# Order of the work rewoven, one more turn on TensorE, bf16 parts made by GpSimd, in an attention and FFN kernel

## The chip, the cores and the metric

One core of a Trainium2 chip. The metric is the device time of one execution in microseconds, the median over runs of the same program.

## The reference

`x` is 2 x 1024 tokens of 128 channels. All is float32.

```python
xn = layernorm(x)                                   # no gain, no bias, eps 1e-5
# attention, 8 heads; queries and keys have 3 channels a head, values 16
q3, k3 = (xn @ Wq.T), (xn @ Wk.T)                   # (b, t, h, 3)
v = xn @ Wv.T                                       # (b, t, h, 16)
scores = q3 . k3 * scale + (q3 . dirs) (k3 . dirs)  # dirs: a fixed unit vector a head
scores = where(causal, scores, -inf)
attn = softmax(scores) @ v;  attn_out = attn @ Wo.T
# FFN, 128 -> 512 -> 128, with ternary weights and a low-rank term
h = xn @ (ternary(w_fc) * s_fc).T + gate * (xn @ v_.T @ fast_b.T @ u.T)
out = x + attn_out + (relu(h) ** 2) @ (ternary(w_proj) * s_pj).T
```

## The kernel before

The 2048 tokens are four **quarters** of 512 (quarter q, half of a batch). The attention runs in eight **chunks** c: one batch, one group of four heads, one block of 512 queries (`CHUNKS`). In the order of `CHUNKS`, chunks 0, 1, 6 and 7 have queries in the first half of their batch (four key tiles, all on the diagonal), chunks 2 to 5 in the second half (eight key tiles, the last four on the diagonal). Quarters 0 and 1 are closed by chunks 1 and 3, quarter 3 by chunk 5 and quarter 2 by chunk 7.

For queries and keys, f32 values are split into three bf16 parts (high, middle, low), which are spread with repeats into rows of the SBUF tile `X` (18 copies of 288 elements in all by GpSimd, line L426); `X` is turned into `QK`, in which the rows of a head lie along the partitions, and one bf16 matmul of 32 rows gives scores of nearly f32 exactness. For quarter 0 TensorE and ScalarE turn it (items `rows`), for quarters 1 to 3 a DMA transpose on SyncE's queue (L355). The split of a later quarter before the change: ScalarE casts PSUM to the high part (L695), VectorE subtracts that from PSUM into an f32 rest in SBUF (L544), GpSimd casts the rest to the middle part (L415) and subtracts for the low one (L416).

For each chunk, TensorE makes the scores a first time with queries along the partitions (`max`, L922) and VectorE takes the row minima of the negated scores (L588 whole, L591 with the causal mask); GpSimd splits these maxima into three bf16 parts and writes them into X beside the queries (`prep`, L464 to L467). X of the chunk's queries is then turned once more (`maxT`): for chunks in `TURNED` by four matmuls with the identity into a PSUM bank (L933) and a ScalarE copy (L726), for the others by a DMA transpose on SyncE (L364). After it TensorE makes the scores with keys along the partitions (`st`, L950), which have the maximum subtracted already; ScalarE applies relu on the diagonal block (`late`, L743) and exp (L757), GpSimd cuts the diagonal block (`causal`, L454), and TensorE multiplies with V (`pv`, L973) into one bank. VectorE and GpSimd then normalise (`oT` L615, `norm` L444), VectorE turns (`oB` L627), and TensorE adds the attention's projection (L993, `y`) to the FFN's (`hid`, L791) in the same bank; VectorE adds x (L634) and SyncE sends the result (out_y, L372). FFN: `ffn`/`ffn2` (L897, L902), relu on ScalarE (L737), `square` on GpSimd (L434). `ternary` (L407 to L410) makes ternary weights on GpSimd, item 0 for w_fc and item 1 for w_proj.

**The order** of all this is one list, `ORDER`. It is written out by hand in the string `WEAVE`: each letter stands for the next item of the stream with that letter in `streams()` (M maxima, A `st`, O `late`, G exp, D `causal`, P `pv`, B `hid`, Y outputs, R `prep`, T `maxT`, I `split`, L `spread`, J ternary 1, S square, n `norm`, E rows, K an idle matmul on zeros). Every engine and SyncE walk through the list and issue, in order, what is theirs; semaphores hold an item until its inputs are there. PSUM has three banks of ring `v` (maxima, weights, turns, FFN output) and two double banks of ring `a` (`st`, `qkv`, `ffn`, xT); units take the banks of their ring in the order of the list.

SyncE's part of the list, before the change, is: rows 1, maxT 1, rows 2, maxT 2, rows 3, maxT 3, maxT 4, y of quarter 0 (first half), maxT 5, y of quarter 0 (second half), maxT 6, y of quarter 1 twice, maxT 7, y of quarter 3 twice, y of quarter 2 twice.

## Time and profile before

| | |
|---|---|
| time, median of 3 runs | 167.89 us (167.42 to 167.95) |
| the profiled execution | 167.61 us, span 165.8 us |
| mean granted TensorE clock | 0.986 |
| TensorE busy | 150.2 us (91%) |
| VectorE busy | 127.1 us (77%) |
| ScalarE busy | 124.1 us (75%) |
| GpSimd busy | 70.7 us (43%) |
| chain that ended last | TensorE 50%, ScalarE 25%, VectorE 7%, issue 7%, DMA 4%, SyncE 3% |

The profile is of one execution. Times are us from the start of the span unless marked ns. A row of an order of time gives start, duration, engine, line, operation, output<-input, form, count, and in brackets how long the engine had been idle before it and what released it. PE is TensorE, PEld its weight loads, DVE VectorE, ACT ScalarE, POOL GpSimd, SPq SyncE's queue. PEclk is the granted clock, 1.00 for 2.4 GHz and 0.50 for 1.2 GHz.

### The profile page before, as it was taken

To read this page: it belongs to the slowest core of one execution; us is meant where nothing else is said; L and a number is where in the kernel's file an instruction comes from. 1 tells how busy PE (TensorE), PEld (TensorE's weight loads), DVE (VectorE), ACT (ScalarE), POOL (GpSimd) and SP (SyncE) were. 2 spreads that over 40 slices of the span, in tenths; PEclk is the share of its full clock that TensorE was granted. 3 is DMA by queue.
4 is the path that set the end of the run, shared out by engine and by line. 5 is a ranking of instruction groups with operands and counts; after the bars stand their busy time and mean duration, and the time that the engine had idled before them with its cause. 6 is when DMAs were issued, how large, how long until landed. Compare 5 with 4: busy or idle time off the path is not lost.

```text
span 165.8 us, 3297 instructions
## 1 busy us (share of the span) xinstructions
PE 150.2 (91%) x1105; PEld 64.2 (39%) x1109; DVE 127.1 (77%) x423; ACT 124.1 (75%) x222; POOL 70.7 (43%) x126
## 2 busy tenths in 40 slices
PE   6999899999999998999899989998499999869992
PEld 2464543523232423213132122234163255655682
DVE  5887899899999999999999979995386873111152
ACT  0888793589789879887899897887399989656700
POOL 4064029649777996157003830045016333411420
PEclk9999999999999999999999999999999999987998
DMA  3850000601042101501000100000202000210022
GB/s 94 202 177 0 6 2 2 124 0 32 4 86 44 32 0 30 101 0 31 4 0 0 34 4 2 0 4 0 63 0 54 14 0 0 62 37 2 0 67 65
DMA packets 16621, 5.71 MB, mean 34 GB/s; under 512 B 11292, under 2 KB 16476, under 8 KB 16604
## 3 DMA queue, kind: packets, MB, share of 16 engines
q1 hardware_dynamic: 16208, 5.34, 14.0%
q8 instruction: 9, 0.15, 0.4%
q10 hardware_dynamic: 396, 0.16, 0.4%
q14 instruction: 8, 0.07, 0.1%
HBM read 1.96 MB, written 1.05 MB: 18 GB/s over the span
## 4 chain that ended last, share of the span: by engine, by line
PE 50%; ACT 25%; DVE 7%; issue 7%; DMA 4%; SPq 3%; ACTq 1%; POOLq 0%; POOL 0%; DVEq 0%
ACT Pr L757 18%; PE obank L973 8%; PE vbank L791 8%; PE vbank L922 7%; PE abank L950 6%; PE abank L897 5%; PE abank L902 5%; DVE vbank L591 5%; ACT abank L743 4%; PE obank L798 3%; DMA QK<-X 3%; PE abank L878 3%; ACT r L737 2%; PE vbank L993 2%; DMA v_sb<-in_L_ffn_v 1%
## 5 line engine op out<-in xcount | busy, mean ns | idle before, releaser
L757 ACT ACTIVATE Pr<-abank 128x1024 f32<-128x1024 f32 (+3 forms) x96 | 74.8, 815 | 13.1 <-PE abank L950 7.1
L591 DVE CUSTOM_DVE_ANT_0 vbank<-vbank,mask_row 128x128 f32<-128x128 f32 (+3 forms) x128 | 59.0, 523 | 10.0 <-PE vbank L922 8.3
L922 PE MATMUL vbank<-QK 32*128 32x512 bf16 (+2 forms) x192 | 40.1, 328 | 1.0 <-DVE pm L591 0.7
L588 DVE TENSOR_REDUCE pm<-vbank 128x1 f32<-128x512 f32 x64 | 39.7, 682 | 1.5 <-PE vbank L922 0.9
L973 PE MATMUL obank<-Pr,V 128*32 128x512 f32 (+3 forms) x384 | 39.7, 498 | 0.1
L454 POOL TENSOR_SCALAR_AFFINE_SELECT Pr<-Pr 128x512 f32<-128x512 f32 x32 | 20.3, 638 | 40.4 <-ACT Pr L757 40.2
L950 PE MATMUL abank<-QK 32*128 32x512 bf16 (+3 forms) x192 | 30.1, 333 | 8.0 <-DMA QK<-X 5.1
L743 ACT ACTIVATE abank<-abank 128x256 f32<-128x256 f32 x64 | 23.7, 376 | 7.8 <-PE abank L950 7.4
L922 PEld LDWEIGHTS vbank<-QK 32*128 32x128 bf16 x192 | 11.7, 91 | 35.7 <-issue 16.6
L950 PEld LDWEIGHTS abank<-QK 32*128 32x128 bf16 x192 | 8.4, 91 | 31.1 <-ACT Pr L757 18.2
L791 PE MATMUL vbank<-w2T,r 128*128 128x128 f32 x128 | 18.6, 298 | 0.2 <-DVE pm L591 0.2
L591 DVE DVE_READ_ACCUMULATOR2_ANT pm<- 128x1 f32 x128 | 18.1, 142 | 0.0
L791 PEld LDWEIGHTS vbank<-w2T,r 128*128 128x128 f32 x128 | 16.3, 203 | 2.2 <-issue 0.9
L434 POOL TENSOR_TENSOR r<-r 128x1024 f32<-128x1024 f32 x8 | 15.1, 1895 | 0.2
L798 PE MATMUL obank<-mask_row 128*128 128x512 bf16 x43 | 13.8, 422 | 1.5 <-POOL mask_row L386 1.3
L444 POOL TENSOR_TENSOR on<-oT,inv 128x256 f32<-128x256 f32 x8 | 5.0, 622 | 21.3 <-DVE inv L618 21.3
L615 DVE STREAM_TRANSPOSE oT<-obank 128x512 f32<-128x512 f32 x8 | 5.7, 713 | 8.9 <-PE obank L973 8.9
L973 PEld LDWEIGHTS obank<-Pr,V 128*32 128x32 f32 x384 | 8.3, 109 | 10.7 <-issue 8.5
L737 ACT ACTIVATE r<-abank 128x1024 f32<-128x1024 f32 x8 | 8.2, 1024 | 4.2 <-PE abank L902 4.2
L897 PE MATMUL abank<-xnT,w1T 128*128 128x512 f32 x16 | 8.9, 638 | 0.4 <-ACT Pr L757 0.2
L634 DVE TENSOR_TENSOR xn<-vbank,x_sb 128x256 f32<-128x256 f32 x8 | 3.3, 415 | 7.4 <-PE vbank L993 7.4
L902 PE MATMUL abank<-xnT,w1T 128*128 128x512 f32 x16 | 9.0, 645 | 0.0
(111 smaller groups left out, 125.4 us busy)
## 6 DMA issues: line engine op xcount, KB each, us to landing
x_sb<-in_L_attn_x SPq DMA_DIRECT2D x4, 256.0 KB, 3.5
out_y<-xn SPq DMA_DIRECT2D x8, 128.0 KB, 1.9
wfc_sb<-in_L_ffn_w_fc SPq DMA_DIRECT2D x1, 256.0 KB, 3.6
wpj_sb<-in_L_ffn_w_proj SPq DMA_DIRECT2D x1, 256.0 KB, 2.8
QK<-X SPq DMA_TRANSPOSE x10, 2.4
k_sb<-in_consts SPq DMA_DIRECT2D x1, 64.0 KB, 2.8
Wv_sb<-in_L_attn_Wv ACTq DMA_DIRECT2D x1, 64.0 KB, 3.4
Wo_sb<-in_L_attn_Wo ACTq DMA_DIRECT2D x1, 64.0 KB, 3.8
```

What stands on the lines that cost most here:

```text
L454: nc.gpsimd.affine_select(diagonal, diagonal, [[0, HG], [1, P]], ALU.is_ge, 0.0, base=0, channel_multiplier=-1).then_inc(causal_done, 1)
L588: last = nc.vector.tensor_reduce(out=least, in_=s_n, op=ALU.min, axis=AX.X)
L591: last = nc.vector.tensor_tensor_reduce(out=s_n, in0=s_n, in1=mask_row[:, CH - keys:CH], scale=1.0, scalar=3.0e38, op0=ALU.add, op1=ALU.mi ...
L743: nc.scalar.activation(scores, scores, ACT.Relu).then_inc(bounded, 1)
L757: nc.scalar.activation(Pr[:, n % PSLOTS, 2 * pair:2 * pair + 2, 0:cols], src[:, :, 0:cols], ACT.Exp, scale=-1.0).then_inc(free(unit), 1)
L791: nc.tensor.matmul(o[:, at:at + P], r2[:, j, t:t + P], w2T[:, j, :], start=j == 0 and at == 0, stop=False)
L798: nc.tensor.matmul(obank[:, :], zeros[:, 0:P], zeros, start=True, stop=True)
L897: nc.tensor.matmul(o[:, 0, :], w1T[:, j * P:(j + 1) * P], xnT[:, q * CH:(q + 1) * CH], start=True, stop=True)
L902: nc.tensor.matmul(bank(unit)[:, 1, :], w1T[:, j * P:(j + 1) * P], xnT[:, q * CH:(q + 1) * CH], start=True, stop=True).then_inc(full(unit), 1)
L922: last = nc.tensor.matmul(o[:, at:at + keys], QK[r, quarter(b, chunk), 0, g, q0:q0 + P], QK[r, quarter(b, half), 1, g, 0:keys], start=True ...
L950: last = nc.tensor.matmul(o[:, n, 0:cols], QK[r, quarter(b, j // TPC), 1, g, k0:k0 + P], QK[r, quarter(b, chunk), 0, g, first:CH], start=T ...
L973: last = nc.tensor.matmul(obank[32 * h:32 * h + 32, first:CH], V[:, b * TPB + j, HG * g + h, :], Pr[:, n % PSLOTS, h, 0:cols], start=step ...
```

## The change

- `TURNED` gains chunk 7: its maxima are turned by four matmuls and a ScalarE copy, no DMA.
- For quarters 1 to 3 ScalarE copies queries and keys from PSUM to the f32 rest in SBUF; GpSimd casts it to the high part and subtracts (two instructions more a quarter, in its chain), and then goes on as before. VectorE's subtraction goes, and V's copy by ScalarE (L708) has no wait for it.
- `WEAVE` is another order of the same 653 items. SyncE's part becomes: rows 1, maxT 1, maxT 2, rows 2, rows 3, maxT 3, maxT 4, maxT 5, y of quarter 0 (first half), y of quarter 0 (second half), maxT 6, y of quarter 1 twice, y of quarter 3 twice, y of quarter 2 twice.
- TensorE from chunk 5's last maxima matmul to its first scores, before: st, pv 4.3, st, two max, hid, two st, hid, two max, st, y, st, pv 4.4 (4.3 and 4.4: steps 3 and 4 of chunk 4). After: st, pv 4.3, st, two max, st, hid, st, hid, st, one max, st, y, one max.
- TensorE from chunk 6's first scores to chunk 7's: before, the other seven st, hid of quarter 1 three times, pv 5.6 and 5.7, y, pv 6.0, y, one hid of quarter 3. After: two max, hid of quarter 1 (all four now), st, pv 5.6, 5.7, st, hid, st, hid, st, y, maxT 7, hid, two st, hid 3, y, st. Chunk 7's last maxima are the two max.
- GpSimd, before, from chunk 1's prep: squares 1 and 2, causal 0.0, square 3, causal 0.1, spread 2, further causal items, square 4, prep 2, ternary 1, three causal, split 3, spread 3, norm 0. After: split 2 ahead of prep 1; from it square 0, ternary 1, spread 2, causal 0.0 and 0.1, square 1, causal 0.2, prep 2, four causal items, square 2, split 3, causal 1.3, norm 0, spread 3, square 3. The last square, ahead of causal 5.0 before, comes between causal 6.0 and 6.1.
- Idle matmuls: 47 before and after; ahead of the first chunk's maxima 27 before and 23 after, ahead of chunk 2's 32 and 28, ahead of quarter 3's xT 33 and 39.

```diff
--- before.py
+++ after.py
@@ -100,7 +100,7 @@
 
 
 
-TURNED = (0,)
+TURNED = (0, 7)
 
 
 def own(c):
@@ -163,12 +163,12 @@
 
 
 WEAVE = """
-KKKKKKKKNKKWKKNCNNWKKXWFUQKNKKKIKKLNUKEVKFKKKNCKKMNMNEKKMMNUMMXKJKMMNMQHNMMVIMHMMXMMLHMMRHEMMQTVMMHMMHSAMOIKMG
-MMHRMMHMAMMSKSOGXMMKKAMOGMHMMAOGMHMMKMAAMDKOKGMMOAOKKSDMGKMAKTGAMOGMLDKMKMAOKGOGDAMMKSKAMODGMMOPMEAMGAOMPGMORJ
-DMAGAOOPGTPGDPMMAQMAMVPDMIMAMAMPLAMMJMAMMAPMAEnMPAMMHPnOMGAMOGHMMMPMAAMOMGOPAGMOMPGMAORDMMAOGPMGMAOSHDMGTAMDHM
-MMAADMMPAMMAMPAMMAMPPAPMMMAOPGAMOMMGAOPMnGDMAPOMGMRAOPDGAMOMMGAOSPGADMMOGTADMAPMAMPAMMAMPHPMMMAHPMMAAMPMAMMMOA
-GMPMOMAGPMAMMDOBGAOGYnRAOBOMGMGAOYGTAODPGAAMMDMPPDAMPMPMnABAMABAMYMAPAROMSMGAPMMAPOGMOMGDAOPMGDAOMPGAOTMMGMAPD
-OAGBOGMAOAYBOBMGGADPPDPROAGYAOGPABOGOAYDTGOAGOGBAOADOBGGBAOPDAPnPGAOGDOYDPBGAPPAOnGDOABYOGGYPDPBPnYBBYY
+NKKKKKNKWKCKKKKKNWKKNXWUFQNILKUKKVKEKKNNKEKKCNMMFNUKJMMHMNHMXMKMMQMMMHNMVMHMXKMMMQMMNVIHMLEMRITHMMKAMKMOHRMGMM
+KHMMSAKKMOKMJKMAMGAKMLOGKKMMODAKGMOHGMAOMMDHGMSMKTMKXMMAKOKGAMKDAMKOMMGOAMKKGAMKMKMOMGAOMRGOPDGMAMOAMPGDOMGMTA
+APODPMMODSGGAQPMVMMIAPAMAMPMMDAPAMPnMEAMMPHAMMHMPMAAMOMLOMSPGGMADEAMOMMnGOPGAMMSOMAPOGMMGMAROHMGMAOHMTDGMJMAAM
+DMPMAMMDAPMAMMAPPAPMMnMAPAMAMMPMOMOGAMGPMOAGOARDMOMGGPAMMOMADPGAMOTGOGMADAMMPMDAMAMPPAMMMAMHAPMHMMPAMAMMPMAMMO
+PGOMGAOMGPADMMABOYGAROGBAOMGDOAOTDYGGMAAMMPMAMDPMAMPPAMnMSAMBAMRMPABAOYAGPnAOMMMGPTSOAMPMGMOAYPMMGOADGAOOGDGPP
+DAAMMOMBOGAGDOPPGRAOBABGDOAYGOGTBSAAOBPYODGGAOADOPGPnGAABODOGBAGPOGPAYOPBDGYAOAYBGnDOAPPDPOGGDPPnBBYBYY
 """
 
 
@@ -411,7 +411,9 @@
                 elif item[0] == "split" and item[1]:
                     q = item[1]
 
-                    pool.wait_ge(res_ready, q + 1)
+                    pool.wait_ge(hi_ready, q + 1)
+                    link(nc.gpsimd.tensor_copy(bf16_part(q, 0), rest(q)))
+                    link(nc.gpsimd.tensor_tensor(rest(q), rest(q), bf16_part(q, 0), ALU.subtract))
                     link(nc.gpsimd.tensor_copy(bf16_part(q, 1), rest(q)))
                     nc.gpsimd.tensor_tensor(bf16_part(q, 2), rest(q), bf16_part(q, 1),
                                             ALU.subtract).then_inc(lo_ready, 1)
@@ -535,14 +537,11 @@
                                                 ALU.subtract, ALU.mult).then_inc(xn_ready, 1)
                 elif item == ("weights", "wqk"):
                     nc.vector.tensor_copy(wall[:, C:VQK], filled(item)[:, 0:2 * NQ]).then_inc(free(item), 1)
-                elif kind == "qkv":
-                    q = item[1]
-                    src = qkv_view(item)[:, :, C:VQK].rearrange("p t (s c) -> p t s c", s=2 * G) if q else qk_rest()
-
-                    dve.wait_ge(hi_ready, q + 1)
-
-                    nc.vector.tensor_tensor(rest(q) if q else src, src, bf16_part(q, 0),
-                                            ALU.subtract).then_inc(res_ready, 1)
+                elif item == ("qkv", 0):
+                    dve.wait_ge(hi_ready, 1)
+
+
+                    nc.vector.tensor_tensor(qk_rest(), qk_rest(), bf16_part(0, 0), ALU.subtract).then_inc(res_ready, 1)
                 elif item == ("split", 0):
                     dve.wait_ge(mid_ready, 1)
                     nc.vector.tensor_tensor(bf16_part(0, 2), qk_rest(), bf16_part(0, 1),
@@ -692,7 +691,9 @@
                     else:
                         filled(item)
                         src = qkv_view(item)[:, :, C:VQK].rearrange("p t (s c) -> p t s c", s=2 * G)
-                    nc.scalar.copy(bf16_part(q, 0), src).then_inc(hi_ready, 1)
+
+
+                    nc.scalar.copy(rest(q) if q else bf16_part(q, 0), src).then_inc(hi_ready, 1)
                 elif kind == "v":
                     q = item[1]
                     unit = ("qkv", q)
@@ -703,7 +704,6 @@
                         act.wait_ge(ones_ready, 2)
                         src = filled(unit)[:, 0, :].rearrange("p (n h d) -> p n h d", n=TPC, d=HD)
                     else:
-                        act.wait_ge(res_ready, q + 1)
                         src = qkv_view(unit)[:, :, 0:C].rearrange("p n (h d) -> p n h d", d=HD)
                     nc.scalar.copy(V[:, q * TPC:(q + 1) * TPC, :, 0:HD], src).then_inc(free(unit), 1)
                 elif item == ("split", 0):
```

## Rows read from the trace of the kernel before

**Rows 1.** Busy time by stage: window; length, busy us (x instructions); PEclk, DMA share, GB/s.

```profile
core 0: us, PE busy (x) PEld busy (x) DVE busy (x) ACT busy (x) POOL busy (x), PEclk, DMA share, GB/s
...
35.00:50.00 15.00, 14.61 (x73) 4.54 (x72) 14.86 (x42) 13.04 (x22) 12.68 (x18) 1.00 0.19 38
50.00:65.00 15.00, 13.92 (x122) 5.09 (x122) 14.72 (x39) 13.10 (x23) 13.38 (x22) 1.00 0.09 18
...
118.20:134.10 15.90, 15.63 (x147) 5.87 (x147) 12.65 (x49) 14.32 (x21) 4.84 (x9) 1.00 0.07 18
134.10:144.40 10.30, 10.30 (x91) 7.14 (x89) 3.59 (x10) 9.00 (x20) 4.13 (x10) 1.00 0.04 13
```

**Rows 2.** Order of time, around the first wait of TensorE for a turn.

```profile
111.80 0.27 POOL L467 TENSOR_TENSOR X<-nres,X 128x16 bf16<-128x16 f32 x1
...
114.06 0.23 PE L950 MATMUL abank<-QK 32*128 32x128 bf16 x2
...
114.22 1.06 PE L973 MATMUL obank<-Pr,V 128*32 128x512 f32 x8
...
115.19 0.40 SPq L372 DMA_DIRECT2D out_y<-xn  x1
...
115.64 1.21 SPq L364 DMA_TRANSPOSE QK<-X  x1
...
118.21 0.40 PE L950 MATMUL abank<-QK 32*128 32x512 bf16 x4 [2.93 <-DMA QK<-X]
```

**Rows 3.** Order of time around the second wait, and the clock (window of TensorE alone).

```profile
135.85 2.05 PE L791 MATMUL vbank<-w2T,r 128*128 128x128 f32 x16
...
139.87 0.28 POOL L467 TENSOR_TENSOR X<-nres,X 128x16 bf16<-128x16 f32 x1
...
144.09 1.20 SPq L364 DMA_TRANSPOSE QK<-X  x1
...
146.64 0.40 PE L950 MATMUL abank<-QK 32*128 32x512 bf16 x4 [2.21 <-DMA QK<-X]
...
146.97 3.23 PE L791 MATMUL vbank<-w2T,r 128*128 128x128 f32 x16
...
148.00:149.00 1.00, 1.00 (x7) 0.50 0.00 0
```

**Rows 4.** Order of time, the turn of chunk 0 by TensorE and ScalarE.

```profile
30.41 0.39 PE L933 MATMUL vbank<-k_sb,X 128*128 128x128 bf16 x4
...
30.84 0.59 ACT L726 CAST QK<-vbank 128x512 bf16<-128x512 f32 x1
```

**Rows 5.** Order of time of ScalarE: start and end of chunk 6, last exp of chunk 7.

```profile
135.70 0.65 ACT L743 ACTIVATE abank<-abank 128x256 f32<-128x256 f32 x2 [0.22 <-PE abank L950]
...
143.87 0.38 ACT L757 ACTIVATE Pr<-abank 128x256 f32<-128x256 f32 x1
...
156.57 0.67 ACT L757 ACTIVATE Pr<-abank 128x256 f32<-128x256 f32 x2
```

**Rows 6.** By source line: duration ns min/median/max, first and last start us.

```profile
L544 DVE TENSOR_TENSOR r<-abank,r x3: 354/357/358, 23.2 to 58.9; 128x192 f32<-128x192 f32 x3
...
L415 POOL CAST r<-r x3: 344/344/345, 23.7 to 60.6; 128x192 bf16<-128x192 f32 x3
...
L416 POOL TENSOR_TENSOR r<-r x3: 563/564/566, 24.1 to 61.1; 128x192 bf16<-128x192 f32 x3
...
L426 POOL COPY X<-r x18: 433/566/622, 24.8 to 63.9; 128x288 bf16<-128x288 bf16 x18
```

**Rows 7.** Order of time of GpSimd, and what waits for it.

```profile
36.39 3.75 POOL L434 TENSOR_TENSOR r<-r 128x1024 f32<-128x1024 f32 x2
...
51.86 1.06 PE L973 MATMUL obank<-Pr,V 128*32 128x512 f32 x8
...
53.83 1.27 POOL L407 TENSOR_TENSOR on<-on 128x512 f32<-128x512 f32 x1
...
61.77 2.77 POOL L426 COPY X<-r 128x288 bf16<-128x288 bf16 x6
...
72.02 8.44 DVE L588 TENSOR_REDUCE pm<-vbank 128x1 f32<-128x512 f32 x13
```

## The prediction

> **What bounds the kernel now.** I read the stage table first. From 35 to 65 us three engines are nearly full together: between 35 and 50 us TensorE is busy 14.61 of 15.00 us and VectorE 14.86, between 50 and 65 us VectorE 14.72 and GpSimd 13.38 [rows 1]. VectorE makes the row maxima there, and goes on with them to 110 us. After 118 us VectorE thins out (12.65 of 15.90, then far less), and TensorE carries the time: 15.63 of 15.90 us and 10.30 of 10.30 us [rows 1]. In such a stretch a wait of TensorE goes straight to the end.
>
> Then I looked for those waits, by the chain of waits and the order of time. There are two long ones, both for a DMA that turns an X tile into QK.
>
> The first: GpSimd ends the maxima of chunk 5 at 111.80 + 0.27 = 112.07 us, but SyncE issues their turn only at 115.64 us, because out_y of quarter 0, first half, stands ahead of it in SyncE's order, waits for VectorE, and is issued at 115.19 us. TensorE has its next scores only at 118.21 us, after 2.93 us of wait [rows 2]. From issue to scores are 118.21 - 115.64 = 2.57 us.
>
> The second: chunk 7's maxima are ready at 139.87 + 0.28 = 140.15 us; SyncE issues their turn at 144.09 us, behind an out_y, and TensorE goes on at 146.64 us, after 2.21 us [rows 3]. This wait has a second price. In 148 to 149 us the granted clock is 0.50, the lower of the two levels (1.2 of 2.4 GHz), and the sixteen FFN matmuls (L791) in it take 3.23 us where sixteen took 2.05 us at full clock [rows 3]: 1.18 us more. TensorE was full up to 144.4 us and stood still for 2.2 us before the fall. After the first, longer wait that doubling isn't seen: the stage from 118.20 to 134.10 us has clock 1.00 [rows 1]. So I count the clock once.
>
> **The change part by part.**
>
> *Turn of chunk 5 ahead of out_y on SyncE.* The turn can be issued at 112.07 us and serve at 112.07 + 2.57 = 114.64 us. What is late next is TensorE's own order. Before, chunk 4's last scores run at 114.06 us and a PV step from 114.22 to 115.28 us stands before chunk 5's first scores [rows 2]. In the new order that PV step stands behind them, so TensorE is ready at about 114.2 us, and 114.64 - 114.2 = 0.4 us of wait is left. The wait of 2.93 us shrinks to that: -2.5 us (bounds -2.0, if GpSimd or the order before it is later, and -2.9). The out_y transfer, now second, has 50 us to land; nobody waits for it.
>
> *Turn of chunk 7 by TensorE.* One DMA goes, and four matmuls and one ScalarE copy come in. The same turn for chunk 0 is in the trace: four matmuls in 0.39 us and a copy of 0.59 us [rows 4]. Nobody waits for SyncE any more. The maxima are ready 2.5 us or so after their last matmul; in the new order chunk 6's scores, four FFN matmul groups and y come between, and between the turn and its first reader there are two more FFN groups (about 1.1 us each), y and three score pairs, some 3.8 us of TensorE work, against 0.59 us of copy plus at most two queued ScalarE instructions. The wait goes: -2.2 us. The clock's price goes with it: -1.2 us (bounds -0.5, if some fall comes elsewhere, and -1.7, 3.5 us at half rate). The four matmuls lie on the bound engine: +0.4 us (up to +1.0 if the copy counts as well).
>
> Of a TensorE transpose of 128x128 bf16, the Trainium skill ("TensorE: Matmul & The Clock Gate", Part 4: PE-mode transpose) says some 275 ns inside a kernel. Four would be 1.1 us by that, and the time 0.7 us later, 162.9 us; the row has them overlapped in 0.39 us, and this kernel's are plain matmuls with the identity, so the row is taken.
>
> *Is ScalarE the next bound?* Chunk 6's relu and exp run without a gap from 135.70 to 144.25 us, 8.55 us [rows 5]. Chunk 5 took from its first scores at 118.21 us to 135.70 us, 17.5 us [rows 2, 5]. From first scores at about 114.7 us ScalarE needs 17.5 + 8.55 + 0.59 + 8.55 = 35.2 us and ends at 149.9 us, 7.3 us before its present end of 156.57 + 0.67 = 157.24 us [rows 5]. TensorE's gains so far are 2.5 + 2.2 + 1.2 - 0.4 = 5.5 us. ScalarE could follow with 1.8 us to spare; TensorE stays the bound, closely.
>
> *Later parts of queries and keys by GpSimd.* VectorE loses three subtractions of 356 ns, 1.07 us, all inside the stretch in which it is full. The one of quarter 3 (after 50 us) counts whole; the two before 35 us, where I have no row that tells VectorE's bound from TensorE's, half: -0.7 us (bounds 0 and -1.1) [rows 1, 6]. ScalarE's copy now writes f32 instead of bf16, which I cost at nothing, and the PSUM bank comes free without a wait for VectorE. GpSimd gets, three times, the cast (344 ns, as its own cast L415) and a subtraction with an f32 result. The nearest row is L416, 564 ns with a bf16 result; from the squares, 3.75 us for two of 1024 elements, 192 elements would be 0.35 us [rows 6, 7]. I take 0.5 us, so 0.9 us for each quarter with the chain of semaphores. Behind it on GpSimd stand the spread (L426), the causal masks and the maxima of the next chunk; who waits are SyncE's turn of the quarter and the PV steps. Quarter 3's spread ends at 61.77 + 2.77 = 64.5 us, and chunk 4's first maxima, which need its turn, come at 72.02 us [rows 7]. That leaves 7.5 us for a transfer of which a smaller one took 2.57 us to its reader, so 0.9 us is hidden there. Cover gone, it would cost at most its own 0.9 us a quarter.
>
> The projection's ternary work (four instructions in a chain, the first 1.27 us, 5.1 us if all are as long [rows 7]) moves from behind chunk 2's maxima to before quarter 2's spread. With one square less in that part, GpSimd has in 35 to 65 us 26.1 + 1.8 - 1.9 = 26.0 of 30 us [rows 1, 6, 7]. From 36.39 us there stand a square (1.9), the ternary work (5.1) and a spread (2.8) before the first mask (0.6): it is there at about 46.8 us, and the first PV step comes at 51.86 us [rows 7]. No cost; one is a rival below.
>
> A rule of the skill speaks against this part: GpSimd shares its SBUF interfaces with VectorE and contends with VectorE instructions of two SBUF inputs or in a two-port mode ("GPSIMD Engine Reference", Key points). L416 took 563 to 566 ns all three times, but the spread's copies 433 to 622 ns [rows 6], so the trace leaves room for it; its result is the slower rival.
>
> *The rest of the order.* As many fillers as before, fewer of them ahead of the first maxima and more in chunk 2's. The start is bound by the same chain to the first maxima, so 0 us, bounds -1.0 and +1.5, since every join of three full engines is new. For joins in the tail that don't fit as well as they did in 118 to 144 us, I add +0.5 us (0 to 2), by the 0.39 and 1.08 us that TensorE lost in 35 to 50 and 50 to 65 us [rows 1].
>
> **The sum.** -2.5 - 2.2 - 1.2 + 0.4 - 0.7 + 0.5 = -5.7 us. The span 165.8 becomes 160.1 us. The profiled run took 167.61 us, 1.8 us more than its span, and lay 0.28 us under the median of 167.89: 160.1 + 1.8 + 0.3 = 162.2 us.
>
> **Rivals.**
>
> 1. The middle gives part back: joins at their upper bounds (+2 us over the 0 and 0.5 that I took). For it speaks that three engines are full from 35 to 110 us; against, that VectorE has less to do. 164.2 us.
>
> 2. The turn by TensorE comes late: its copy stands in ScalarE's full queue, or GpSimd is late with the maxima, TensorE waits as before and the clock falls again. Then 2.2 + 1.2 us are not won: 165.6 us. Against it stand 3.8 us of work between turn and reader.
>
> 3. The middle wins too: VectorE's full 1.1 us and 1.0 us from the leaner start, no loss at joins: 162.2 - 0.4 - 1.0 - 0.5 = 160.3 us; with the clock's bound of -1.7 it is 159.8 us.
>
> 4. Slower: GpSimd becomes the bound of 35 to 65 us, by contention. If its instructions stretch by the ratio of the spread's copies, 622 / 433 = 1.44, its 26.0 us become 37.4 us in a stretch of 30, and all behind its masks moves by 7.4 us: 162.2 + 7.4 = 169.6 us. It decides from a stretch of 30 / 26.0 = 1.15, and makes the kernel slower than before from (30 + 5.7) / 26.0 = 1.37. The equal durations of L416 speak against it.
>
> 5. The change doesn't do what it says: SyncE's queue still blocks. In the new order chunk 5's turn stands ahead of the first out_y, chunk 6's behind out_y of quarter 0 but 30 steps ahead of its reader; that leaves it next to nothing. About 167.5 us.
>
> **How the numbers follow.** Forecast (160.7 to 163.5 us): 0.66. Rival 1 (up to 165.0): 0.14. Rival 2: 0.05. Rival 3: 0.09. Rival 4: 0.03. Rival 5 and no change: 0.03. The range 159.8 to 164.8 us takes in the forecast, nearly all of rival 1 and two thirds of rival 3, about 0.85. A difference of 0.3% is about what a measurement of this kernel can tell from none. Faster: 0.66 + 0.14 + 0.05 + 0.09 = 0.94; same 0.03; slower 0.03.
>
> **What would show it.** First wait: chunk 5's scores at most 0.5 us after the PE work before them, no SP line between 112 and its turn. Second: no wait for a DMA after 130 us, four matmuls at L933 a second time, clock 1.00 in every slice up to the last. VectorE: one subtraction at the old L544 instead of four, and chunk 5's last maxima some 0.7 us earlier than 110.4 us. GpSimd: six new instructions of 0.35 to 0.6 us, and no PV step waiting for a mask before 65 us. Wrong would be: a new wait of TensorE of over 1 us anywhere, GpSimd durations above those of before, a clock of 0.50 in another place, or a last maximum of chunk 5 later than 111 us.

## The result, and the profile after

The changed kernel takes 159.69 us (median of 4 runs, 159.43 to 160.19); the kernel before, on the same chip, 167.92 us (167.42 to 169.38). The ratio is 0.95, 95% interval 0.9435 to 0.9565. Here and below a median is over all executions, while a ratio leaves out those over 1.5% above the fastest of their kernel, which count as a slower state. The forecast was 162.2 us with a range from 159.8: the direction was right, and the time fell 0.1 us below the range. The profiled execution took 159.43 us with a span of 157.7 us, where the sum had 160.1 us. So 8.1 us of span went, and the sum had 5.7.

The first lines of the page of after, TensorE's clock in 40 slices (9 stands for 0.9 or more), and the only line that the view of TensorE's waits has after 100 us (line waited for: us in total, times, longest):

```profile
span 157.7 us, 3312 instructions
...
PE 148.4 (94%) x1113; PEld 63.7 (40%) x1113; DVE 126.9 (80%) x420; ACT 124.1 (79%) x223; POOL 73.0 (46%) x132
...
PEclk9999999999999999999999999999999999999999
...
PE abank L950 <- ACT Pr L757: 0.9, 3, 0.5
```

TensorE's busy time fell by 1.8 us (from 150.2) and its idle time from 15.6 to 9.3 us. No wait for a DMA is left after 100 us, and the granted clock is 1.00 in every stage of the table below. In the kernel before, the same view had 5.1 us for the DMA of QK, in two waits [rows 2, 3].

Order of time of after, at the places of [rows 2] and [rows 3] (start, duration, engine, line):

```profile
110.50 0.27 POOL L469 TENSOR_TENSOR X<-nres,X 128x16 bf16<-128x16 f32 x1
...
110.79 1.68 SPq L364 DMA_TRANSPOSE QK<-X  x1
...
114.09 0.67 PE L950 MATMUL abank<-QK 32*128 32x512 bf16 x4
...
114.46 9.30 SPq L372 DMA_DIRECT2D out_y<-xn  x2
...
136.52 0.39 PE L933 MATMUL vbank<-k_sb,X 128*128 128x128 bf16 x4
...
137.31 0.58 ACT L726 CAST QK<-vbank 128x512 bf16<-128x512 f32 x1
...
139.53 0.45 PE L950 MATMUL abank<-QK 32*128 32x128 bf16 x4
```

The turn of chunk 5 is issued 0.02 us after its maxima are whole, and its scores follow other work with nothing in brackets, which is to say without a wait. Chunk 7's turn is four matmuls and a copy that ends at 137.89 us, 1.6 us before the scores that first read it.

To see where the time went, I cut both spans at the same events: the last maxima of chunk 0 and of chunk 5, the first scores of chunks 5 and 7, the end of the last PV step. Before, from chunk 4's last maxima on (columns as in [rows 1]):

```profile
90.50:110.56 20.06, 18.65 (x155) 4.51 (x153) 18.42 (x51) 17.33 (x28) 6.39 (x11) 1.00 0.04 8
110.56:118.21 7.65, 4.72 (x40) 2.97 (x41) 3.73 (x19) 4.16 (x11) 3.10 (x8) 1.00 0.15 36
118.21:146.64 28.43, 25.96 (x236) 13.03 (x237) 16.95 (x59) 23.32 (x40) 10.17 (x19) 1.00 0.10 24
146.64:158.76 12.12, 12.12 (x113) 7.87 (x113) 1.82 (x4) 7.76 (x16) 3.13 (x5) 0.86 0.01 2
```

After:

```profile
90.67:109.26 18.59, 17.33 (x149) 4.48 (x145) 18.30 (x52) 16.50 (x26) 4.01 (x9) 1.00 0.05 9
109.26:114.09 4.83, 4.14 (x38) 2.96 (x34) 2.95 (x15) 4.44 (x11) 2.46 (x7) 1.00 0.16 31
114.09:139.53 25.44, 25.22 (x240) 13.06 (x238) 16.94 (x62) 23.23 (x40) 13.29 (x21) 1.00 0.08 22
139.53:151.04 11.51, 11.51 (x124) 7.22 (x123) 2.96 (x6) 8.38 (x19) 4.84 (x8) 1.00 0.12 35
```

| stage | before, us | after, us | difference |
|---|---|---|---|
| start to chunk 0's maxima | 25.93 | 26.03 | +0.10 |
| to chunk 4's maxima | 64.57 | 64.64 | +0.07 |
| to chunk 5's maxima | 20.06 | 18.59 | -1.47 |
| to chunk 5's scores | 7.65 | 4.83 | -2.82 |
| to chunk 7's scores | 28.43 | 25.44 | -2.99 |
| to the last PV step's end | 12.12 | 11.51 | -0.61 |
| to the end | 7.04 | 6.66 | -0.38 |
| span | 165.8 | 157.7 | -8.1 |

Two things stand out. The stretch of 64.6 us in which VectorE lost two of its three subtractions (the first, at 23.2 us [rows 6], lies ahead of chunk 0's maxima) is as long as before. And chunk 5's maxima, of which the prediction said nothing apart from VectorE's 0.7 us, came 1.5 us sooner after chunk 4's, while chunk 4's came 0.5 us later after chunk 3's (19.07 against 18.58 us).

### The profile page after: what moved, and what is told of

The parts are those of the page before. It is cut to its first block, busy times and chain, and to the rows that moved or that the text cites. A ratio compares the mean times of both kernels' runs of the same rounds, so it can differ in the third digit from the quotient of the medians.

```text
span 157.7 us, 3312 instructions
## 1 busy us (share of the span) xinstructions
PE 148.4 (94%) x1113; PEld 63.7 (40%) x1113; DVE 126.9 (80%) x420; ACT 124.1 (79%) x223; POOL 73.0 (46%) x132
## 4 chain that ended last, share of the span: by engine, by line
PE 56%; ACT 24%; DVE 12%; issue 6%; ACTq 0%; POOL 0%; DVEq 0%; POOLq 0%
ACT Pr L757 19%; PE vbank L922 8%; PE vbank L791 8%; PE obank L973 8%; PE obank L798 8%; DVE pm L587 6%; PE abank L897 5%; PE abank L902 5%; ACT abank L743 5%; PE abank L950 4%; DVE vbank L590 4%; PE vbank L993 2%; PE abank L878 2%; PE abank L849 2%; PE vbank L829 1%
## 5 line engine op out<-in xcount | busy, mean ns | idle before, releaser
L590 DVE CUSTOM_DVE_ANT_0 vbank<-vbank,mask_row 128x128 f32<-128x128 f32 (+3 forms) x128 | 58.9, 524 | 6.7 <-PE vbank L922 6.5
L922 PE MATMUL vbank<-QK 32*128 32x512 bf16 (+3 forms) x192 | 40.8, 329 | 2.2 <-DVE pm L590 0.9
L587 DVE TENSOR_REDUCE pm<-vbank 128x1 f32<-128x512 f32 x64 | 39.4, 682 | 0.6 <-PE vbank L922 0.5
L973 PE MATMUL obank<-Pr,V 128*32 128x512 f32 (+3 forms) x384 | 38.6, 495 | 0.2 <-issue 0.2
L950 PE MATMUL abank<-QK 32*128 32x512 bf16 (+3 forms) x192 | 30.6, 331 | 2.0 <-ACT Pr L757 1.6
L590 DVE DVE_READ_ACCUMULATOR2_ANT pm<- 128x1 f32 x128 | 18.3, 143 | 0.0
L798 PE MATMUL obank<-mask_row 128*128 128x512 bf16 x47 | 16.4, 430 | 1.3 <-POOL mask_row L386 1.3
L791 PE MATMUL vbank<-w2T,r 128*128 128x128 f32 x128 | 17.6, 284 | 0.0
L950 PEld LDWEIGHTS abank<-QK 32*128 32x128 bf16 x192 | 8.6, 91 | 21.3 <-ACT Pr L757 15.6
L791 PEld LDWEIGHTS vbank<-w2T,r 128*128 128x128 f32 x128 | 15.3, 191 | 1.9 <-issue 1.2
```

The lines of the kernel that those rows point to most:

```text
L587: last = nc.vector.tensor_reduce(out=least, in_=s_n, op=ALU.min, axis=AX.X)
L590: last = nc.vector.tensor_tensor_reduce(out=s_n, in0=s_n, in1=mask_row[:, CH - keys:CH], scale=1.0, scalar=3.0e38, op0=ALU.add, op1=ALU.mi ...
L791: nc.tensor.matmul(o[:, at:at + P], r2[:, j, t:t + P], w2T[:, j, :], start=j == 0 and at == 0, stop=False)
L798: nc.tensor.matmul(obank[:, :], zeros[:, 0:P], zeros, start=True, stop=True)
L922: last = nc.tensor.matmul(o[:, at:at + keys], QK[r, quarter(b, chunk), 0, g, q0:q0 + P], QK[r, quarter(b, half), 1, g, 0:keys], start=True ...
L950: last = nc.tensor.matmul(o[:, n, 0:cols], QK[r, quarter(b, j // TPC), 1, g, k0:k0 + P], QK[r, quarter(b, chunk), 0, g, first:CH], start=T ...
```

## The experiments

My theory after the result: two waits for a turn and the clock behind them make most of it; the split by GpSimd frees VectorE, which had 0 to 1.1 us to give; the new order around the chunks does the rest. The rivals: one of the parts does nothing, or does it only together with another. Each part was done alone in the kernel before, or undone in the changed one. Ratios are against the kernel before on the same chip as the experiment. That kernel's median was 168.85, 168.61 and 169.76 us on the three chips, with spans from 165.5 to 169.4 us; why it spreads so far is part of what follows. Only the last group of experiments had the changed kernel beside it on the same chip, so small differences are read from stages that begin at chunk 0's maxima: up to chunk 5's maxima, profiles of kernels with the same order and the same split agree within 0.06 us.

**Turn of chunk 5 ahead of the first out_y, alone** (kernel before, two letters exchanged):

```diff
-...YnRAOBOMGMGAOYGTAODPGAA...
+...YnRAOBOMGMGAOTYGAODPGAA...
```

> The kernel before, with one thing changed: SyncE issues the DMA turn of chunk 5 ahead of the first out_y. Theory (a wait of TensorE in the late part goes straight to the end): the wait of 2.93 us ahead of chunk 5's first scores goes, because the turn lands at about 114.6 us and TensorE is free only at 115.3 us; span 162.9 us, 2.9 us less, about 165.0 us of time. Rival (given back later, since chunk 7's turn is still held by out_y and ScalarE is nearly full): less than 1.5 us of gain, and the wait ahead of chunk 7's scores grows over 2.2 us.

Measured: 165.24 us (163.05 to 166.0), ratio 0.972 [0.9632, 0.9807]; the theory's 165.0 us. The order of time of its profiled execution:

```profile
112.07 1.19 SPq L364 DMA_TRANSPOSE QK<-X  x1
...
114.19 1.06 PE L973 MATMUL obank<-Pr,V 128*32 128x512 f32 x8
...
115.16 0.39 SPq L372 DMA_DIRECT2D out_y<-xn  x1
115.18 0.47 PE L950 MATMUL abank<-QK 32*128 32x512 bf16 x4
```

SyncE gives out the turn at 112.07 us, the very time that the prediction named, and the whole wait of 2.93 us is gone: scores at 115.18 instead of 118.21 us. The clock, TensorE alone, in the second wait and behind it:

```profile
143.00:144.00 1.00, 0.38 (x4) 0.53 0.00 0
144.00:145.00 1.00, 1.00 (x8) 0.50 0.06 16
...
149.00:150.00 1.00, 1.00 (x10) 0.56 0.00 0
```

Here it is at its lower level (1.2 GHz) for nearly seven microseconds from the end of the second wait on, over six of them with TensorE full. In the profiled execution of the kernel before it was so for 3.4 us. The same wait has different prices in different executions: four executions of this one kernel had spans of 161.3, 162.8, 164.0 and 164.3 us with mean clocks of 0.996, 0.987, 0.978 and 0.979.

**Turn of chunk 7 by TensorE, alone** (kernel before with `TURNED = (0, 7)`):

> The kernel before, with one thing changed: chunk 7's maxima are turned by TensorE, in the old order. Theory: the wait of 2.21 us goes and with it the half clock, of which I now count 1.5 us (1.18 us on the FFN matmuls, the rest on the scores and PV of the same stretch), against 0.4 us for four matmuls: 3.3 us less, 164.6 us of time, clock 1.00 in every slice up to 150 us. Rival (the copy stands late in ScalarE's queue, since in this order it comes after chunk 6's exp, close to its reader): at least 1 us of wait stays and the gain is under 2.3 us.

Measured: 166.27 us (165.41 to 167.72), ratio 0.9872 [0.98, 0.9945]. The DMA's wait goes and a smaller one comes:

```profile
142.87 0.39 PE L933 MATMUL vbank<-k_sb,X 128*128 128x128 bf16 x4
...
143.30 0.59 ACT L726 CAST QK<-vbank 128x512 bf16<-128x512 f32 x1 [1.48 <-PE vbank L933]
...
143.78 0.60 ACT L757 ACTIVATE Pr<-abank 128x512 f32<-128x512 f32 x1
...
144.44 0.23 PE L950 MATMUL abank<-QK 32*128 32x128 bf16 x2 [1.18 <-ACT Pr L757]
```

ScalarE stands for 1.48 us at its copy, which waits for the turn, with an exp in its queue behind it whose input is there. TensorE needs the bank that this exp empties, and stands for 1.18 us. That is the rival "the turn by TensorE comes late", in the old order, at a third of the price that I gave it. Neither expectation was quite met: 1.2 us of wait stayed, and the median fell by 2.6 us, more than the rival's 2.3 and less than the theory's 3.3.

**The split by GpSimd, alone** (the diff's parts at L411, L535, L692 and L703, in the old order, with turns as before):

> The kernel before, with one thing changed: the later parts of queries and keys made by GpSimd, in the old order. Theory after the result: VectorE's saved instructions before 35 us bring nothing and the third 0.3 us, so the time is 0.3 us lower at most. Rival (the prediction's term, VectorE bound in the middle): 0.7 to 1.1 us lower. Rival (GpSimd contention): slower, and GpSimd's copies take over 622 ns.

Measured: 168.23 us (166.96 to 170.06, 10 runs), ratio 0.998 [0.9936, 1.0023]. The interval alone would leave room for 1 us; the stages don't. From chunk 0's to chunk 5's maxima it takes 84.57 us, the kernel before 84.63. What VectorE waits for from 26 us to chunk 5's maxima, in this kernel:

```profile
DVE vbank L590 <- PE vbank L922: 1.2, 3, 0.7
DVE pm L587 <- PE vbank L922: 1.2, 3, 0.5
```

and in the kernel before:

```profile
DVE pm L588 <- PE vbank L922: 0.9, 2, 0.5
DVE r L544 <- ACT r L695: 0.6, 1, 0.6
DVE vbank L591 <- PE vbank L922: 0.3, 1, 0.3
```

Two subtractions (0.7 us) and the wait of 0.6 us ahead of one of them went out of this stretch, and VectorE's waits for TensorE grew from 1.2 to 2.4 us: what was taken from VectorE came back as time in which it waits for maxima matmuls. TensorE, which feeds it, is busy 79.9 of the 84.6 us itself, VectorE 81.1 before and 80.6 now. VectorE was the fuller of the two and still not what set the pace.

**The changed kernel without the split** (everything else of the change kept):

> The changed kernel without the GpSimd part: VectorE makes the three subtractions again. Theory (VectorE had waits for TensorE in that stretch which the removed instructions only lengthened): the same within 0.3 us, 159.7 us. Rival (in the new order VectorE is the bound): 0.7 to 1.1 us slower, and each chunk's maxima end later by 0.36 us a quarter.

Measured: 161.8 us (161.49 to 162.14), ratio 0.9622 [0.9564, 0.968], 1.7 and 2.1 us over the two medians of the changed kernel (160.08, below, and 159.69). Both expectations missed: it is more than the rival's 0.7 to 1.1 us. So the part that is worth nothing alone is worth nearly 2 us in the new order. Its order of time, in quarter 3's split:

```profile
60.09 0.36 DVE L544 TENSOR_TENSOR r<-abank,r 128x192 f32<-128x192 f32 x1 [0.67 <-ACT r L695]
...
60.36 0.71 DVE L615 STREAM_TRANSPOSE oT<-obank 128x512 f32<-128x512 f32 x1
60.48 0.58 ACT L708 COPY V<-abank 128x512 f32<-128x512 f32 x1 [0.42 <-DVE r L544]
...
61.17 1.06 PE L973 MATMUL obank<-Pr,V 128*32 128x512 f32 x8 [0.93 <-ACT V L708]
```

and of the changed kernel:

```profile
58.03 0.71 DVE L614 STREAM_TRANSPOSE oT<-obank 128x512 f32<-128x512 f32 x1
...
58.65 0.59 ACT L708 COPY V<-abank 128x512 f32<-128x512 f32 x1
...
58.87 1.06 PE L973 MATMUL obank<-Pr,V 128*32 128x512 f32 x8
```

VectorE stands 0.67 us for ScalarE's cast, V's copy on ScalarE 0.42 us for VectorE's subtraction, and TensorE 0.93 us ahead of the PV step. The view names V's copy as what released the PV step; the kernel's semaphores say otherwise. The PV step is the first of chunk 1: it needs V of quarter 0, long there, and the bank of the sums, which VectorE's `oT` of chunk 0 empties. That `oT` ends at 61.07 us, as V's copy does. In the old order it stands ahead of quarter 3's subtraction in VectorE's queue, in the new one behind it, and so behind its wait for ScalarE. In the changed kernel, without the subtraction, it runs at 58.03 us and the PV step at 58.87, while V's copy is still under way. From chunk 2's to chunk 3's maxima this kernel takes 20.29 us, the changed one 19.32; 0.45 us more lie between the first two chunks' maxima. That is 1.4 of the 1.7 us by which the time from chunk 0's maxima to the end grew (131.7 to 133.4 us); the rest I have not placed.

This doesn't make the split a gain over the kernel before. From chunk 0's to chunk 4's maxima the stages are:

| | without the split | with the split |
|---|---|---|
| old order | 64.57 us | 64.51 us |
| new order | 66.05 us | 64.64 us |

The new order up to there loses 1.5 us without the split, and with it stands where the old order stood. The split repairs what the order does; both together are worth nothing in this part. No run has the old order up to chunk 4, the new one behind it, and no split; by these stages I estimate that it would be as fast as the first kernel of "Where in the order" below.

**All three parts in the old order** (changed kernel with the order of before, chunk 5's turn ahead of out_y):

> The three parts together in the old order, only with chunk 5's turn ahead of the first out_y. Theory (the parts add up, and the rest of the change's 8.2 us is in the new order): 2.9 + 3.3 + 0.3 = 6.5 us less than before, 161.4 us, some 1.7 us more than the changed kernel. Rival (the three parts make it all): within 0.5 us of the changed kernel's 159.7 us. Rival (they don't add up without the new order, ScalarE being full from 118 us on): 163 us or more.

Measured: 162.33 us (162.15 to 162.64), ratio 0.9632 [0.9586, 0.9677], span 160.8, 0.7 us over the sum of the prediction. It has the wait of 1.2 us behind ScalarE's copy, and from chunk 0's to chunk 5's maxima 84.6 us. The remaining 2.3 to 2.6 us (162.33 to 160.08 and 159.69, on other chips) are the order's; from chunk 0's maxima to the end it is 134.4 against 131.7 us, half of the difference before chunk 5's maxima and half behind them.

**Where in the order.** Two kernels with all parts and half of each order, joined at chunk 4's last maxima. There the two orders differ by six items, among them one PV step of chunk 3 that the new order has ahead of the join; the tails are adapted so that each item comes once. Old order first, then the new:

> All three parts; the order of before up to the end of chunk 4's maxima (about 90 us), the new order after it. Theory (the middle before 90 us gained nothing, all the rest of the gain is in the new order after it): 159.7 us, within 0.4 us of the changed kernel. Rival (the new order's start and middle carry part of it): 160.5 us or more.

Measured: 160.05 us (159.64 to 161.7), ratio 0.9542 [0.9474, 0.961], span 158.4. New order first, then the old:

> All three parts; the new order up to the end of chunk 4's maxima, then the order of before with chunk 5's turn ahead of the first out_y. Theory: as the three parts in the old order, 162.3 us, with chunk 5's last maxima 19.9 to 20.1 us after chunk 4's and 1.2 us of wait for ScalarE ahead of chunk 7's scores. Rival (the new start matters): 161.5 us or less.

Measured: 163.13 us (162.76 to 163.26), ratio 0.9704 [0.9655, 0.9752], span 161.2. So nearly all that the order gives lies behind chunk 4's maxima. (The second kernel was expected at 162.3 us and is 0.8 us over it, but from chunk 0's maxima to the end it takes 134.5 us and all three parts in the old order 134.4, so the difference lies in the start. The first takes 132.0 us and the changed kernel 131.7; those 0.4 us need both halves of the order.) From there to chunk 5's maxima the new tail takes 19.06 us and the old 20.05, and after chunk 5's maxima 48.5 against 49.8 us. The first of these is VectorE's stage, and its waits show the difference. New order first, old tail:

```profile
L587 DVE TENSOR_REDUCE pm<-vbank 128x1 f32<-128x512 f32 x16 | 10.1, 681 | 1.2 <-PE vbank L922 1.2
```

Old order first, new tail:

```profile
L587 DVE TENSOR_REDUCE pm<-vbank 128x1 f32<-128x512 f32 x16 | 10.0, 685 | 0.4 <-PE vbank L922 0.4
```

The same 16 maxima in 10 us, with 1.2 us of standing still ahead of them in the one and 0.4 in the other (in the changed kernel itself none). TensorE's busy time in this stage goes the same way: 18.64 us with the old tail, 17.93 with the new one. But the number of matmuls is 153 in both, so it isn't that work was moved out: as many matmuls stand in another order and overlap more. Which place in the order matters was not tried by itself and stays open. In the changed kernel TensorE is busy 17.33 us with 149 matmuls, as half a PV step more is done before, in the stage up to chunk 4's maxima. So the two stages are better read together:

| from the last maxima of chunk | 0 to 3 | 3 to 5 |
|---|---|---|
| kernel before | 45.99 us | 38.64 us |
| old order, then new | 45.92 us | 37.65 us |
| new order, then old | 45.54 us | 39.11 us |
| changed kernel | 45.57 us | 37.66 us |

The new tail is worth 1.0 us behind the old order and 1.4 us behind the new one. The new start of the order is worth 0.4 us, and only the new tail keeps them.

The second difference (48.5 against 49.8 us) is the wait of 1.2 us for ScalarE, which the new order doesn't have: there TensorE has work for all of the 2.6 us between the turn's end at 136.91 us and the scores that need the copy, and ScalarE comes to the copy without a wait.

**What the clock costs.** Eight matmuls of zeros, added to the bank of the attention's sums in the second wait of the kernel before, so that TensorE doesn't stand still; the sums stay as they are:

```diff
+                    if item[1:] == (7, 0, 0):
+                        for _ in range(8):
+                            nc.tensor.matmul(obank[:, :], zeros[:, 0:P], zeros, start=False, stop=False)
```

> The kernel before; in the wait for chunk 7's turn TensorE makes eight matmuls on zeros that add nothing to the PV bank (about 0.24 us each, 1.95 us in a wait of 2.2 us). Theory (the wait has a second price, the half clock, which differs between executions: spans of the kernel before ran from 165.6 us at a mean clock of 0.99 to 168.2 us at 0.97): with the wait kept and the clock held, about 164.4 us of span and 166.2 us of time, 2.5 us under the kernel before on this chip, mean clock 1.00, and a spread under 0.5 us. Rival (the fall costs only the 1.2 us that the prediction took): 1.2 us under before. Rival (the clock falls whatever TensorE does there): no difference.

Measured: 167.92 us (167.01 to 169.23, 10 runs), ratio 0.9985 [0.9945, 1.0025]. A miss. TensorE's windows:

```profile
120.00:122.00 2.00, 2.00 (x23) 0.50 0.00 0
...
148.00:150.00 2.00, 1.66 (x16) 1.00 0.00 0
```

The clock held after the second wait as it should, but in this execution it had fallen after the first, where the profile of before showed none. It was no exception: nine of the ten executions had mean clocks of 0.98 to 0.99. So the same was done in both waits, with 11 and 8 matmuls:

> The kernel before with 11 matmuls of zeros added to the bounds bank in the first wait and 8 in the second, so that TensorE is at work in both (the output is unchanged). Theory (after either wait TensorE's clock falls to half for some microseconds, in some executions after the one, in some after the other, in some after both, and that is the spread of the kernel before, whose spans go from 165.5 to 168.4 us): clock 1.00 in every stretch after start-up, spans of 164.3 to 165.0 us in all executions, 1.5 to 3 us under the median of the kernel before on the same chip, and a spread below 0.5 us. Rival (the spread has another cause, or the falls cost nothing at the end): the median within 0.5 us of the kernel before, its spread as wide.

Measured: 166.09 us (165.67 to 166.43), ratio 0.9808 [0.9737, 0.9878]; the kernel before had a median of 169.76 us beside it. The four spans are 163.9 to 164.7 us at mean clocks of 0.998 to 1.00. The last stage but one of the profiled execution, where the kernel before has 12.12 us at a clock of 0.86:

```profile
146.80:157.30 10.50, 10.50 (x112) 6.72 (x112) 1.82 (x4) 7.62 (x16) 3.12 (x5) 1.00 0.01 2
```

The turns come no sooner: chunk 5's scores come at 118.47 us, chunk 7's at 146.80. Only the clock differs. So the clock alone is worth 1.6 us in the execution on which I had predicted (12.12 to 10.50), and 3.7 us in the medians of this chip. It also is the spread of the kernel before: the four spans here lie within 0.8 us, and that kernel's longest span, 169.4 us, is 5.0 us over the 164.4, where its mean clock of 0.968 makes 5.4 us of lost clock, as an estimate.

**Undoing each turn in the changed kernel.** The first out_y ahead of chunk 5's turn again:

> The changed kernel with one pair of steps exchanged: the first out_y of the late part goes ahead of chunk 5's turn again, as in the kernel before. Theory (SyncE's queue stands on out_y until y is ready at 114.46 us, and the turn behind it is issued after that): chunk 5's scores start near 117.4 us instead of 114.09, a wait of about 3 us of TensorE for the DMA comes back, and the end moves by 3 us, with a half clock after the wait in some executions: 162.5 to 164 us. Rival (the new order around the turn fills the wait with other matmuls, so that the place of the turn is worth little there): at most 1 us over the changed kernel, 160 to 161 us.

Measured: 165.22 us (164.14 to 165.86), ratio 0.9751 [0.9662, 0.984].

```profile
114.96 0.39 SPq L372 DMA_DIRECT2D out_y<-xn  x1
115.40 1.20 SPq L364 DMA_TRANSPOSE QK<-X  x1
...
117.95 0.40 PE L950 MATMUL abank<-QK 32*128 32x512 bf16 x4 [3.21 <-DMA QK<-X]
```

One exchange of two letters costs 5.1 us over the changed kernel on the same chip: 3.2 us of wait, and a clock of 0.50 behind it (its mean from 118 to 134 us is 0.89). It is more than the theory's upper end of 164 us, by the clock again: it lost 1.7 us, and the theory had that only for some executions.

Chunk 7's maxima turned by the DMA again (`TURNED = (0,)`, new order kept):

> The changed kernel with chunk 7's maxima turned by the DMA again, its new order kept. In the changed kernel SyncE's queue gives out y at 137.17 us and chunk 7's scores start at 139.6. Theory: the DMA turn is held behind that out transfer until about 137.6 us and takes about 2.5 us to land, so chunk 7's scores start at about 140.1 to 140.5 instead of 139.6, TensorE waits 0.5 to 0.9 us for the DMA and its clock stays at 1.00, while the four turning matmuls (0.4 us) go: 160.0 to 160.5 us, that is, at most 0.8 us over the changed kernel. Rival (in the new order the DMA's turn would cost what it cost in the kernel before): a wait of 2.2 us and a half clock after it in some executions, 162 to 163 us.

Measured: 160.38 us (160.08 to 163.54), ratio 0.9465 [0.9383, 0.9548].

```profile
137.23 0.38 SPq L372 DMA_DIRECT2D out_y<-xn  x1
...
137.65 1.20 SPq L364 DMA_TRANSPOSE QK<-X  x1
...
140.19 0.39 PE L950 MATMUL abank<-QK 32*128 32x512 bf16 x2 [0.64 <-DMA QK<-X]
```

As the theory had it: the turn is held until out_y is away, 3.6 us after its maxima are whole (134.02 us), lands 2.54 us later, and TensorE waits 0.64 us. In the new order, the turn by TensorE is worth 0.3 us at the median of the four executions, and nothing measurable without the longest (the middle one of the other three took 160.12 us). The longest had a mean clock of 0.989 and took 163.54 us; that clock accounts for some 1.8 of its 3.4 us, and the rest is open. Not tried is a simpler cure in the old order: the DMA turn of chunk 7 kept and put ahead of the out_y, as was done for chunk 5.

**The changed kernel again**, beside the last three on one chip:

> The changed kernel itself, on the same chip as the other three for a direct comparison: 159.4 to 160.2 us, clock 1.00 throughout, no wait of TensorE for a DMA after 100 us, chunk 5's last maxima at 109.3 us (up to 0.8 us later where start-up before the first maxima is longer).

Measured: 160.08 us (159.66 to 160.38), ratio 0.9456 [0.9371, 0.954], clock 1.000 in all four executions.

## Why the prediction was wrong by 2.4 us of span, point by point

- *Turn of chunk 5 ahead of out_y*, taken at -2.5 us: right in mechanism, and the wait went whole, 2.93 us. The step "0.4 us of wait is left" failed: done alone, the turn lands behind the PV step, and the scores run at 115.18 us straight after it; in the changed kernel the turn leaves 1.3 us sooner, since chunk 5's maxima do. 0.4 us.
- *Turn of chunk 7 by TensorE*, -2.2 and +0.4 us: the sizes were right (wait gone, four matmuls in 0.39 us). But the term was booked on the wrong part: with the DMA kept in the new order the wait is 0.64 us. Most of the 2.2 us came from where chunk 7's first scores stand among the other work. The turn by TensorE in the old order makes a wait of 1.2 us that I had argued away by counting TensorE's work between turn and reader (3.8 us; it is 2.6 us in the changed kernel) without looking at what ScalarE holds back behind the copy.
- *The clock*, -1.2 us: mis-sized. I took the difference of sixteen matmuls, which lie only in part in the stretch at half clock, as the whole [rows 3]. The windows of the kernel before, one by one, had the answer:

```profile
147.00:148.00 1.00, 1.00 (x11) 0.81 0.06 16
...
149.00:150.00 1.00, 1.00 (x6) 0.50 0.00 0
150.00:151.00 1.00, 1.00 (x7) 0.50 0.00 0
```

  With 148 to 149 us from [rows 3] that is 0.19 + 3 x 0.50 = 1.7 us of lost clock, on an engine that is full. The kernel with held clock confirms it: from chunk 7's scores to the last PV step's end it takes 10.50 us instead of 12.12. I had 1.7 us as a bound and took the smaller value. 0.5 us. "After the first wait that doubling isn't seen, so I count the clock once" was true of one execution and false of others.
- *VectorE's three subtractions*, -0.7 us: wrong as a term. One subtraction is left, as said, but alone the split changes nothing (84.57 against 84.63 us up to chunk 5's maxima), because VectorE then waits for TensorE. The prediction took VectorE's busy time in a full stretch as its price, and of the three subtractions only two lie in it. The bound of 0 was in the text.
- *GpSimd*: right. Two new instructions a quarter, the cast at 343 ns and the subtraction with an f32 result at 563 to 567 ns (I had taken 500), the spread's copies as before:

```profile
L415 POOL CAST r<-r x3: 343/343/343, 23.9 to 58.8; 128x192 bf16<-128x192 f32 x3
...
L416 POOL TENSOR_TENSOR r<-r x3: 563/567/567, 24.3 to 59.2; 128x192 f32<-128x192 f32 x3
...
L428 POOL COPY X<-r x18: 426/564/622, 26.1 to 64.2; 128x288 bf16<-128x288 bf16 x18
```

  Nothing of the slower rival came: no group of GpSimd's instructions grew by more than 0.01 us. Of the contention with VectorE that the Trainium skill states ("GPSIMD Engine Reference", Key points) these rows show none, but they test it little: VectorE's two large groups, the maxima of L587 and L590, read their scores from PSUM and so have no two inputs in SBUF. What the split is worth in the new order lies in what I had given no price: VectorE's `oT` stood behind a subtraction that waits for ScalarE, and V's copy on ScalarE behind that.
- *The rest of the order*, 0 in the middle and +0.5 us for joins: this step failed most. Nothing was lost at the joins of the changed kernel: 0.4 us were won up to chunk 3's maxima and 1.0 us from there to chunk 5's. I had treated a hand-woven order as something that can only cost. By the stages, the part up to chunk 5's maxima is -1.3 us (start included) and not -0.7, and apart from the two waits, the clock and the four matmuls another 0.4 us went. With the 0.5 us this is 1.5 us.

The differences add up: 0.4 + 0.5 + 1.5 = 2.4 us. The measured terms: -2.9 -2.2 + 0.4 - 1.7 (clock) - 1.7 (order) = -8.1 us. The last is what the stages leave (1.3 us up to chunk 5's maxima and 0.4 us behind them), and no run measures it by itself.

Of the rivals, "the middle wins too" came nearest (160.3 us), though not by its mechanism: of its 1.0 us from a leaner start and 0.4 us from VectorE nothing came (the start takes 26.03 against 25.93 us). Of the signs that I named, all but one came out as said; chunk 5's maxima were 1.3 us earlier and not 0.7. The two bounds on which terms of the result lay (2.9 and 1.7 us) were both in the text, and the range left out a third of that rival: with terms that lean the same way, its lower end should have stood at the sum of the bounds: -2.9 - 2.2 - 1.7 + 0.4 - 1.1 - 1.0 = -8.5 us of span, or 159.4 us.

## What to carry to other kernels

Before you price a clock's fall, add up the clock over all windows behind the wait, and keep the engine awake in one experiment: its cost varies from execution to execution, and a profile shows one of them. Look in every in-order queue, SyncE's and ScalarE's alike, for an instruction that waits for something late while the one behind it is ready; one such place was worth 5 us here, and an exchange of two letters mends it. Time taken off the fullest engine was worth nothing here, as the engine that feeds it was nearly full too, so judge a moved operation by the chain that it shortens. Try parts that were made for each other both singly and together, and compare each pair with the kernel before as well: a part can look worth 2 us only because it repairs another.

## What the runs showed of the hardware

- After a wait of 2 to 3 us TensorE's clock fell to half in some executions and not in others, of the same kernel on the same chip, and stayed there for 3.4 us (the kernel before; the one with eight matmuls of zeros; the one with out_y first again; and after both waits in the one with the split alone) or 6.8 us (chunk 5's turn first alone), with the engine full but for the first 0.6 us of the last. That last kernel's four executions had mean clocks of 0.978 to 0.996. The kernel before had spans of 165.5 to 169.4 us by this, at mean clocks of 0.99 to 0.968. In all eight executions of the changed kernel the mean clock was 1.000. After a wait of 0.64 us it fell in one execution of four (mean 0.989) and not in the profiled one; whether that fall followed this wait I can't say, as only the mean is known.
- A DMA transpose of one chunk's queries took 2.54 to 2.57 us from issue to the scores that waited for it in the kernel before (both places) and in the two kernels in which a turn was undone, and 2.45 and 2.46 us in the one with held clock. It isn't always so: chunk 7's took 3.07 us in the kernel with eight matmuls of zeros (145.27 to 148.34 us) and 3.50 us in the one with the split alone (145.65 to 149.15 us). Why, no run shows.
- The start up to chunk 0's maxima took between 25.8 and 26.9 us in different executions, so ends are compared from that event on.
